# GpSimd gathers in bursts of four blocks in the message stage of a graph network

## The chip, the cores and the metric

The kernel runs on one core of a Trainium2 chip. The metric is the device time of one execution in microseconds (us). The kernel before took 2001.14 us (median of three runs, 1994.20 to 2003.65).

## The reference

Two graph layers with a mixture-of-experts layer behind each, on 3125 nodes of 256 numbers. The stage that is changed here is the message passing of the second graph layer. For each of 53,125 edges it takes the source node's row of `y`, multiplies it by weights of the edge, and adds the products up at the destination node:

```python
xg0 = y0[edge_src]
xg1 = y1[edge_src]
mid0 = w_a * xg0 * ea0
mid1 = w_b * jnp.einsum('euc,ec->eu', xg1, ea1) * INV_SQRT3
mid2 = (w_c * xg0)[:, :, None] * ea1[:, None, :]
mid3 = (w_d * ea0)[:, :, None] * xg1
mids = jnp.concatenate([mid0, mid1, mid2.reshape(-1, 3 * MUL), mid3.reshape(-1, 3 * MUL)], axis=1)
agg = jax.ops.segment_sum(mids, edge_dst, num_segments=n)
```

The edges are sorted by destination, so a run of neighbouring edges adds into a few neighbouring nodes.

## The kernel before

The program is a chain of stages that follow each other on all engines: a first summing stage (`sum`), the first node update, the first experts, a table stage that writes `y_dram`, the message stage (`msg`, the function `sum_messages`), the second update and routing, and the second experts.

**Tiles.** The nodes are cut into 25 tiles of 125. The sorted edges are cut into 208 blocks (`NB`) of 256. A block that lies across the border of two tiles belongs to both, so there are 208 + 25 - 1 = 232 pairs of a tile and a block (`NPAIR`). One step of the stage works on two pairs, so there are 116 steps (`NST`). Pair n belongs to block n - t when its tile is the t-th counted from 0. The first pair takes block 0, the last (n = 231, t = 24) block 207; a step uses 208/116 = 1.79 new blocks in the mean.

**A step on the engines.** SP loads the edge weights `w` of the two blocks (L1916), one load a pair. VectorE (DVE in the profile) makes a 0/1 mask of which edge goes to which node (L1993), then the products of gathered rows and weights (L2010, L2012: six instructions), then adds the sums of the step three earlier into `agg` (L2022, two instructions). ScalarE (ACT) scales the mask by the edge attributes, twelve instructions (L1961). TensorE (PE) multiplies masks and products into PSUM, which is the segment sum (L1978, L1982).

**Gathers.** GpSimd (POOL) fetches the rows of `y` that a block needs, with two indirect DMAs of 128 rows of 1 KB for each block (L1940), into a ring of 32 slots (`got`). The two DMAs of a block add 32 to that slot's semaphore `got_in` when they have landed. Behind each block POOL writes a small tile (`rest`, L1945).

**What sets the order.** The loop of each engine is written out by hand, and each engine runs its own list in order. These semaphores matter here:

- `blocks_in` is the number of blocks that have been counted as landed. POOL raises it in `arrived` (L1931 to L1934), after waiting for the blocks' `got_in`. DVE's products of a step wait until it reaches the number that the step needs (L2004).
- `made` is the number of steps whose products are done. POOL waits for it before it issues block b > 7 (L1938): steps 0 to (b - 6)//2 - 1 must be done. SP's loads of `w` wait for it too (L1909).
- `summed` is the number of steps that TensorE has finished. DVE's mask of step s waits for step s - 4 (L1992), its adds for theirs (L2018).

In the kernel before, POOL counts two blocks after it has issued two more: behind block b = 3, 5, 7, ... it waits for blocks b - 3 and b - 2, and it counts the last two at the end (L1946 to L1948).

Of the kernel before, what the change touches and what calls it, by code (L numbers as in the profile page):

```python
# [27 lines left out]
NB = -(-E // SB)  # L28
# [1836 lines left out]
def sum_messages(nc, k):  # L1865


    RING, LAG = 32, 3
    assert NB % 2 == 0
    AHEAD = RING - T  # L1870
    assert LAG + 2 < AHEAD
    RS, MB, ZB, XB = 4, 4, 6, 3
    LAST = NPAIR // 2 - 3
    assert LAST % RS == LAST % MB == 1 and LAST % XB == 2
# [3 lines left out]
    with Phase(nc, "msg") as ph:  # L1878
# [20 lines left out]
        w_in, got_in, blocks_in = ph.sems("w_in", RS), ph.sems("got_in", RING), ph.sem("blocks_in")  # L1899
# [5 lines left out]
        @block.sync  # L1905
        def _(sp):
            for s in range(NST):
                if s >= RS:
                    sp.wait_ge(made, s - RS + 1)  # L1909
                    sp.wait_ge(scaled_made, s - RS + 1)  # L1910
                if s == 1:
                    sp.wait_ge(k.x_put, 32 * (NG - 1))
                for h in range(2):
                    n = 2 * s + h
                    need = sp.value_load(k.pair_need[0:1, n:n + 1], min_val=1, max_val=NB)
                    sp.dma_start(w[s % RS][:, KC * h:KC * h + KC, :].rearrange("p u w -> p (u w)"),  # L1916
                                 k.edge_w[ds((need - 1) * SB, SB), :].rearrange("(p u) w -> p (u w)", u=KC)).then_inc(w_in[s % RS], 16)
            sp.wait_ge(raw_zero, 1)
            w00, w01, w10, w11 = k.L1_gnn_lin2_w00, k.L1_gnn_lin2_w01, k.L1_gnn_lin2_w10, k.L1_gnn_lin2_w11
            for q, (wa, wb) in enumerate([(w00, w11), (w11, w11), (w01, w10), (w10, w10)]):  # L1920
                sp.dma_start(raw[0:MUL, q, 0:MUL], wa).then_inc(raw_in, 16)
                sp.dma_start(raw[MUL:128, q, MUL:128], wb).then_inc(raw_in, 16)
            sp.wait_ge(summed, LAST + 1)
            for i in range(1, NG):
                for a, b in SPANS:
                    sp.dma_start(k.x_sb[a:b, i * G:i * G + G, :], k.x_dram[i * W:i * W + W, :].rearrange("(j p) d -> p j d", p=P)[a:b, :, :])\
                      .then_inc(k.x_back[i], 16)

        @block.gpsimd
        def _(pool):  # L1930
            def arrived(first, second):  # L1931
                for b in (first, second):
                    pool.wait_ge(got_in[b % RING], (b // RING + 1) * 16 * KC)
                pool.sem_inc(blocks_in, 2)  # L1934

            for b in range(NB):
                if b > AHEAD:
                    pool.wait_ge(made, (b - AHEAD + 1) // 2)  # L1938
                for u in range(KC):
                    pool.indirect_dma_start(  # L1940
                        got[:, (b + 1) % RING, u, :, :].rearrange("p k v -> p (k v)"), None, k.y_dram,
                        bass.IndirectOffsetOnAxis(ap=k.block_src[:, b, u:u + 1].bitcast(U32), axis=0)).then_inc(got_in[b % RING], 16)
                if b >= 1:
                    pool.wait_ge(rested, b)
                pool.memset(rest[:, :], 0.0).then_inc(rested, 1)  # L1945
                if b % 2 == 1 and b >= 3:  # L1946
                    arrived(b - 3, b - 2)
            arrived(NB - 2, NB - 1)  # L1948

        @block.scalar  # L1950
        def _(act):
# [517 lines left out]
def build(nc, inputs, out, stop=99):  # L2469
# [8 lines left out]
    with ExitStack() as ctx:  # L2478
# [58 lines left out]
        with ExitStack() as held:  # L2537
            k.agg = held.enter_context(nc.sbuf_tensor("agg1", [128, T, 2 * D], F32))
            k.up_w = held.enter_context(nc.sbuf_tensor("up_w", [128, 4, 128], F32))
            k.x_back = [nc.alloc_semaphore(f"x_back{i}") for i in range(NG)]  # L2540
            sum_messages(nc, k)
            m = Experts(nc, held, "ffn1", 8, 1, 1024, last=True)
            k.wd = held.enter_context(nc.sbuf_tensor("wd", [128, m.n, m.hid // 128, D], F32))
            k.wd_in = nc.alloc_semaphore("wd_in")
            k.row_stored = [nc.alloc_semaphore(f"row_stored{r}") for r in range(HR)]
            update_and_route(nc, k, m)
            m.hold_weights(nc, held)
            pick_slots(nc, k, m, k.L1_ffn_bd)
            run_second_experts(nc, k, m)
# [19 lines left out]
```

## Time and profile before

| what | value |
|---|---|
| runs, median (lowest to highest) | 2001.14 us (1994.20 to 2003.65) |
| profiled execution, span of its instructions | 2413.3 us |
| message stage in the profile, 1248 to 2057 us | 809 us |
| VectorE busy in it | 524.84 us |
| TensorE busy in it | 627.66 us, at 0.84 of the full clock |
| GpSimd busy in it | 441.23 us |

For the profiled execution the page gives the span from its first to its last instruction, and no other time of it; that span is 412.2 us longer than the median of the runs. How to read the views: "busy" is the time in which an engine executes; waits, branches and the issuing of hardware-queue DMAs are not counted. In a timeline each row is an instruction or a merged run of equal ones, with its start, its length, and in brackets the idle time of its engine just before it and what ended that. "issue" there means that the engine waited for nothing that the profile shows, "remote" that the semaphore was raised by an instruction whose record is missing. The clock column is the granted clock of TensorE, 1.00 for 2.4 GHz and 0.50 for 1.2 GHz.

### The profile page before, as it was taken

How to read it: one execution, taken by the hardware profiler on the slowest of the kernel's cores; microseconds unless marked ns; L12 is line 12 of the kernel's file. 1: busy time of each engine (PE TensorE's matmuls, PEld its weight loads, DVE VectorE, ACT ScalarE, POOL GpSimd, SP SyncE). 2: the span in 40 equal slices, each digit the busy share in tenths (PEclk: the TensorE clock that was granted, in tenths of full speed). 3: DMA queues.
4: the chain of work that ended last, by engine and by line, in shares of the span. 5: the costliest groups of instructions: out<-in, count | busy, mean ns of one | idle time of the engine just before them, and what ended most of it. 6: DMA issues, size and time to landing. Idle time of an engine off the chain costs nothing. (4 is left out here: it accounts for less than half of the span.)

```text
span 2413.3 us, 38460 instructions
## 1 busy us (share of the span) xinstructions
PE 1891.3 (78%) x9911; PEld 1517.9 (63%) x9911; DVE 1125.8 (47%) x2791; ACT 1021.4 (42%) x3052; POOL 1104.5 (46%) x1499
## 2 busy tenths in 40 slices
PE   1368787877799858999455877787778789899699
PEld 1245454554466657999335766676767679777588
DVE  3532222222242374544664666565656669431322
ACT  2513343343353532333264555454545557454222
POOL 5547667666700004555375665565655550000243
PEclk7679999889999858999777888887888889999799
DMA  5636556565734026666544554555554553255553
GB/s 150 202 90 198 190 187 198 185 193 187 210 140 138 11 64 201 212 212 215 135 149 147 150 159 140 151 155 145 147 153 144 150 148 107 69 164 177 155 180 129
DMA packets 229197, 376.43 MB, mean 156 GB/s; under 512 B 66081, under 2 KB 114308, under 8 KB 228998
## 3 DMA queue, kind: packets, MB, share of 16 engines
q1 hardware_dynamic: 174820, 222.13, 31.0%
q0 software_dynamic: 52224, 150.15, 20.2%
q8 instruction: 89, 1.46, 0.2%
q10 hardware_dynamic: 1954, 1.79, 0.2%
q14 instruction: 110, 0.90, 0.1%
HBM read 275.38 MB, written 99.57 MB: 155 GB/s over the span
## 5 line engine op out<-in xcount | busy, mean ns | idle before, releaser
L1940 POOL DMA_INDIRECT msg_got<-y_dram,block_src x416 | 412.4, 991 | 293.5 <-DVE msg_prod L2012 139.7
L439 POOL DMA_INDIRECT ffn_w<-xn_dram,block_src x384 | 364.6, 949 | 219.2 <-issue 81.7
L1961 ACT ACTIVATE msg_scaled<-msg_plain,msg_w 128x125 f32<-128x125 f32 x1044 | 314.0, 386 | 280.1 <-DVE msg_plain L1993 234.6
L554 PE MATMUL sum_ps_bank<-ffn_w,sum_onehot 128*125 x928 | 270.5, 419 | 115.6 <-DVE sum_onehot L893 84.3
L554 PEld LDWEIGHTS sum_ps_bank<-ffn_w,sum_onehot 128*125 128x125 f32 x928 | 184.0, 206 | 264.6 <-issue 246.6
L881 DVE TENSOR_TENSOR agg<-sum_ps_bank,agg 125x256 f32 x232 | 98.4, 424 | 432.4 <-PE sum_ps_bank L554 216.5
L541 PE MATMUL sum_ps_bank<-sum_fc,sum_space 128*128 128x512 f32 x416 | 231.9, 644 | 68.9 <-ACT sum_space L639 48.3
L650 ACT ACTIVATE sum_space<-sum_ps_bank,sum_rec 128x128 f32<-128x128 f32 x416 | 131.0, 369 | 330.4 <-PE sum_ps_bank L541 159.5
L1982 PE MATMUL msg_ps_z<-msg_prod,msg_scaled 128*125 128x128 f32 x1416 | 207.5, 293 | 53.7 <-issue 53.0
L1982 PEld LDWEIGHTS msg_ps_z<-msg_prod,msg_scaled 128*125 128x125 f32 x1416 | 198.6, 206 | 72.4 <-issue 64.1
L2022 DVE TENSOR_TENSOR agg<-msg_ps_z,agg 125x512 f32 x232 | 159.4, 687 | 23.9 <-issue 5.2
L1978 PE MATMUL msg_ps_z<-msg_prod,msg_plain 128*125 128x256 f32 x472 | 142.1, 420 | 31.9 <-issue 20.0
L2439 POOL DMA_INDIRECT last_rows<-ffn_rows,ffn_token x32 | 30.8, 963 | 289.2 <-SPq L78 279.7
L1533 ACT ACTIVATE ffn_run_hid<-ffn_run_ps_h,cols 128x128 f32<-128x128 f32 x256 | 73.2, 368 | 178.9 <-issue 134.6
L1993 DVE TENSOR_TENSOR msg_plain<-msg_ps_lanes,pair_dst 128x500 f32<-128x500 f32 x87 | 58.5, 672 | 190.6 <-remote 183.6
L1961 ACT ACTIVATE x_sb<-x_sb 128x125 f32<-128x125 f32 x348 | 104.0, 385 | 93.4 <-DVE x_sb L1993 77.2
L541 PEld LDWEIGHTS sum_ps_bank<-sum_fc,sum_space 128*128 128x128 f32 x416 | 76.0, 205 | 93.5 <-ACT sum_space L639 53.8
L1490 PEld LDWEIGHTS ffn_run_ps_h<-ffn_run_rows_t,ffn_run_w 128*128 128x128 f32 x1024 | 125.9, 194 | 5.0 <-DVE ffn_run_rows_t L1575 1.8
L1490 PE MATMUL ffn_run_ps_h<-ffn_run_rows_t,ffn_run_w 128*128 128x128 f32 x1024 | 126.6, 277 | 1.0 <-DVE ffn_run_rows_t L1575 1.0
L1982 PE MATMUL msg_ps_z<-x_sb,msg_scaled 128*125 128x128 f32 x672 | 100.1, 292 | 29.9 <-issue 29.7
L1504 PE MATMUL ffn_run_ps_r<-ffn_w,ffn_run_hid 128*128 x512 | 121.0, 379 | 0.0
L2012 DVE TENSOR_TENSOR msg_prod<-msg_w,msg_got 128x384 f32<-128x384 f32 x236 | 120.2, 550 | 0.0
(343 smaller groups left out, 3397.9 us busy)
## 6 DMA issues: line engine op xcount, KB each, us to landing
edge_w<-sum_space SPq DMA_DIRECT2D x52, 1040.0 KB
msg_w<-edge_w SPq DMA_DIRECT2D x174, 260.0 KB
ffn_run_w<-in_L_ffn_w SPq DMA_DIRECT2D x64, 512.0 KB
x_sb<-edge_w SPq DMA_DIRECT2D x58, 260.0 KB
ffn_rows<-agg SPq DMA_DIRECT2D x25, 448.0 KB
ffn_w<-in_L_ffn_w SPq DMA_DIRECT2D x16, 512.0 KB, 8.7
wd<-in_L_ffn_Wd SPq DMA_DIRECT2D x8, 1024.0 KB, 8.6
msg_got<-y_dram,block_src POOLq DMA_INDIRECT x416
```

The lines of the kernel that those rows point to most:

```text
L439: pool.indirect_dma_start(got[:, (b + 1) % RING, u, :], None, k.x if b < RAW else k.xn_dram, bass.IndirectOffsetOnAxis(ap=k.block_src[:, b ...
L541: pe.matmul(ps_w[q % WB][:, :, :].rearrange("p u d -> p (u d)"), hid[g % 2][:, b, :], fc2[:, :, :, :].rearrange("p u k v -> p (u k v)"), s ...
L554: last = pe.matmul(ps_sum[n % ZB][0:P, :], onehot[n % OB][:, u, :], got[:, ds(need % RING, 1), u, :].rearrange("p o d -> p (o d)"), start= ...
L650: act.activation(to[:, b, u, 0:128], ps_w[q % WB][:, u, 0:128], ACT.Copy, scale=r[:, b, u, 8:9])
L1490: last = pe.matmul(ps_h[b][c // 4][:, c % 4, :], w1[s][:, q, c * 128:(c + 1) * 128], rows_t[b][:, q, :], start=(q == 0), stop=(q == 1))
L1504: last = pe.matmul(ps_r[b][:, :], hid[b][:, c, :], m.w2[:, ds(e, 1), c, :].rearrange("p o d -> p (o d)"), start=(c == 0), stop=(c == HC - 1))
L1940: pool.indirect_dma_start(got[:, (b + 1) % RING, u, :, :].rearrange("p k v -> p (k v)"), None, k.y_dram, bass.IndirectOffsetOnAxis(ap=k.bl ...
L1961: last = act.activation(scaled[s % MB][:, x, c, :], plain[s % MB][:, c, :], ACT.Copy, scale=w[s % RS][:, c, D + x:D + x + 1])
L1978: pe.matmul(z[0:P, 0:4, :], mask[:, c, :], p[:, c, 0:4, :], start=(u == 0), stop=False, skip_group_check=True)
L1982: last = pe.matmul(z[0:P, 4:6 + x:1 + x, :], by[:, x, c, :], p[:, c, 4 + x:8:3 - x, :], start=False, stop=(x == 2 and u == KC - 1), skip_g ...
L2012: last = dve.tensor_tensor(p[:, at, 3 * q - 2:3 * q + 1, :], v[:, at, q:q + 1, :].to_broadcast([128, KC, 3, MUL]), y[:, :, 1:4, :], ALU.mult)
L2022: dve.tensor_tensor(row(k.agg, tile), ps_z[n % ZB][0:P, :, :].rearrange("p k v -> p (k v)"), row(k.agg, tile), ALU.add)\
```

## The change

POOL's loop now issues four blocks (eight gathers), waits until all four have landed, and counts the four together. The wait and the count behind every second block are gone, and so is the separate count at the end. The gather instructions, their number and their order stay; the semaphore `made` is waited for as before.

```diff
-    RING, LAG = 32, 3
-    assert NB % 2 == 0
+    RING, BURST = 32, 4
+    assert NB % BURST == 0
...
-            def arrived(first, second):
-                for b in (first, second):
+            def arrived(blocks):
+                for b in blocks:
                     pool.wait_ge(got_in[b % RING], (b // RING + 1) * 16 * KC)
-                pool.sem_inc(blocks_in, 2)
+                pool.sem_inc(blocks_in, len(blocks))
...
-                if b % 2 == 1 and b >= 3:
-                    arrived(b - 3, b - 2)
-            arrived(NB - 2, NB - 1)
+                if b % BURST == BURST - 1:
+                    arrived(range(b - BURST + 1, b + 1))
```

On POOL, blocks 6 and 7 and the start of block 8 read as follows in the kernel before. Semaphores are reused from stage to stage and stand here under names of an earlier stage: `sum_consts` and `sum_iota_made` are `got_in` of blocks 2 and 3, `sum_eps_made` and `sum_agg_zero` those of blocks 4 and 5, `sum_r_rstd_done` is `made`, `sum_r_stats_done` is `rested`.

```order
L1940 DMA msg_got<-y_dram,block_src 128x256 [waits sum_consts,sum_iota_made]
L1940 DMA msg_got<-y_dram,block_src 128x256
L1945 MEMSET msg_rest 128x32 [waits sum_r_stats_done]
L1940 DMA msg_got<-y_dram,block_src 128x256 x2
L1945 MEMSET msg_rest 128x32 [waits sum_r_stats_done]
L1940 DMA msg_got<-y_dram,block_src 128x256 [waits sum_eps_made,sum_agg_zero,sum_r_rstd_done]
```

So block 6 waits for blocks 2 and 3, and block 8 waits for blocks 4 and 5 while 6 and 7 are still under way. In the changed kernel the same place on POOL reads as follows; `sum_spare_zero` and `sum_tail_zero` are `got_in` of blocks 6 and 7.

```order
L1940 DMA msg_got<-y_dram,block_src 128x256 x2
L1945 MEMSET msg_rest 128x32 [waits sum_r_stats_done]
L1940 DMA msg_got<-y_dram,block_src 128x256 x2
L1945 MEMSET msg_rest 128x32 [waits sum_r_stats_done]
L1940 DMA msg_got<-y_dram,block_src 128x256 [waits sum_spare_zero,sum_tail_zero,sum_eps_made,sum_agg_zero,sum_r_rstd_done]
```

Block 6 waits for no landing any more, and block 8 waits for the landing of blocks 4 to 7, of which block 7 was issued just ahead of it. There are 52 such places, one behind each burst; in the last one it is the end of POOL's loop that waits.

## Rows read from the trace of the kernel before

**Rows 1.** Busy time by stretch: start:end, length, engines, clock, DMA share, GB/s

```profile
core 0: us, PE busy (x) PEld busy (x) DVE busy (x) ACT busy (x) POOL busy (x), PEclk, DMA share, GB/s
160.00:690.00 530.00, 424.65 (x1563) 271.31 (x1564) 154.25 (x366) 208.92 (x729) 344.37 (x507) 0.93 0.60 189
940.00:1100.00 160.00, 160.00 (x1116) 151.15 (x1116) 86.20 (x282) 49.18 (x172) 86.38 (x86) 1.00 0.66 212
1248.00:2057.00 809.00, 627.66 (x3714) 557.91 (x3714) 524.84 (x1047) 423.57 (x1393) 441.23 (x624) 0.84 0.51 149
1976.00:2045.00 69.00, 69.00 (x509) 65.40 (x509) 66.67 (x136) 53.99 (x182) 3.66 (x6) 1.00 0.40 111
```

**Rows 2.** Waits in the message stage: who, for whom, us in total, times, longest

```profile
DVE msg_plain L1993 <- remote: 183.6, 32, 18.9
POOL msg_got L1940 <- DVE msg_prod L2012: 139.7, 30, 7.6
POOL msg_got L1940 <- DVE x_sb L2012: 59.9, 13, 5.4
POOL msg_got L1940 <- DMA msg_got<-y_dram,block_src: 0.5, 3, 0.2
```

**Rows 3.** Timeline, 1274 to 1278 us: TensorE, ScalarE and GpSimd while gathers run

```profile
1274.03 0.40 ACT L1961 ACTIVATE msg_scaled<-msg_plain,msg_w 128x125 f32<-128x125 f32 x1 [0.99 <-issue]
1274.34 0.95 POOL L1940 DMA_INDIRECT msg_got<-y_dram,block_src  x1 [0.17 <-issue]
1274.74 0.37 PE L1982 MATMUL msg_ps_z<-msg_prod,x_sb 128*125 128x128 f32 x1 [2.52 <-issue]
1277.54 0.37 PE L1982 MATMUL msg_ps_z<-msg_prod,x_sb 128*125 128x128 f32 x1 [2.43 <-issue]
```

**Rows 4.** Mask instructions (L1993) from 1976 us on: ns, first and last start

```profile
L1993 DVE TENSOR_TENSOR msg_plain<-msg_ps_lanes,pair_dst x11: 668/668/679, 1981.4 to 2040.8; 128x500 f32<-128x500 f32 x11
L1993 DVE TENSOR_TENSOR x_sb<-msg_ps_lanes,pair_dst x4: 668/668/679, 1976.7 to 2031.7; 128x500 f32<-128x500 f32 x4
```

**Rows 5.** Waits of GpSimd's gathers in the first stage, 150 to 700 us

```profile
POOL ffn_w L439 <- remote: 56.7, 32, 2.0
POOL ffn_w L439 <- PE sum_ps_bank L554: 33.1, 19, 7.2
```

**Rows 6.** Timeline: first gather, first products, last products, last adds

```profile
1248.67 1.04 POOL L1940 DMA_INDIRECT msg_got<-y_dram,block_src  x1 [3.06 <-POOLq L82]
...
1257.32 0.42 DVE L2010 TENSOR_TENSOR msg_prod<-msg_w,msg_got 128x256 f32<-128x256 f32 x1 [0.89 <-issue]
...
2045.37 0.41 DVE L2010 TENSOR_TENSOR msg_prod<-msg_w,msg_got 128x256 f32<-128x256 f32 x1
...
2055.43 1.53 DVE L2022 TENSOR_TENSOR agg<-msg_ps_z,agg 125x512 f32 x2 [1.37 <-PE msg_ps_z L1982]
```

**Rows 7.** Timeline: GpSimd over four blocks, DVE's release, a later gather

```profile
1604.04 0.95 POOL L1940 DMA_INDIRECT msg_got<-y_dram,block_src  x1 [5.33 <-DVE x_sb L2012]
...
1613.23 0.95 POOL L1940 DMA_INDIRECT msg_got<-y_dram,block_src  x1 [0.30 <-issue]
...
1617.75 1.02 DVE L2012 TENSOR_TENSOR msg_prod<-x_sb,msg_got 128x384 f32<-128x384 f32 x2
...
1619.04 0.95 POOL L1940 DMA_INDIRECT msg_got<-y_dram,block_src  x1 [4.73 <-DVE msg_prod L2012]
...
1842.20 0.95 POOL L1940 DMA_INDIRECT msg_got<-y_dram,block_src  x1 [0.30 <-issue]
```

**Rows 8.** DMA view, 1614.2 to 1617.2 us: GB/s in 40 equal slices

```profile
GB/s 219 218 273 273 55 0 0 0 0 273 0 164 382 273 109 219 164 164 0 0 0 0 0 0 0 0 0 0 0 0 0 0 0 0 0 0 0 218 0 0
```

**Rows 9.** DMA view, 1843.2 to 1846.2 us, behind the gather of 1842.20 us

```profile
GB/s 222 194 250 166 277 387 332 360 333 221 166 221 275 275 166 111 192 301 164 164 164 109 55 0 0 55 0 0 55 0 0 0 0 0 0 0 0 0 218 0
q1 hardware_dynamic: 133, 0.24, 22.9%
```

More of the change, by code:

```diff
@@ L1865, in sum_messages @@
 def sum_messages(nc, k):
-    RING, LAG = 32, 3
-    assert NB % 2 == 0
+    RING, BURST = 32, 4
+    assert NB % BURST == 0
     AHEAD = RING - T
-    assert LAG + 2 < AHEAD
+    assert BURST + 2 < AHEAD
     RS, MB, ZB, XB = 4, 4, 6, 3
```

## The prediction

> **What bounds the kernel now.** I read the busy times by stretch first, to see what the message stage costs and which engine is full there: 809 us, in which no engine is [rows 1]. Then the waits, for the gathers of GpSimd and the masks of VectorE; the reader is to see that waiting for a landing costs GpSimd 0.5 us in the whole stage, while it waits 139.7 + 59.9 = 199.6 us in 43 places for VectorE's products, and that VectorE's longest wait is at the mask, whose only semaphore is `summed` [rows 2]. So in the profile GpSimd is early, and TensorE late. Then the timeline, to see what keeps TensorE: nothing that it waits for. While gathers run, it starts one matmul in 2.80 us (1274.74 to 1277.54) with "issue" ahead of it, and ScalarE sits idle 0.99 us before an instruction in the same way, in the middle of twelve equal ones; GpSimd beside them keeps its even pace [rows 3]. Last the end of the stage, where the gathers are over but all else goes on: TensorE is busy 69 of 69 us at the full clock, and VectorE 66.67 [rows 1]. Its 15 masks from 1976.7 to 2040.8 stand 64.1/14 = 4.58 us apart [rows 4]. A step therefore costs 4.58 us once TensorE is not held; in the stage as profiled it costs 809/116 = 7.0.
>
> That makes one question decide the forecast: is TensorE held in this way in the timed runs too? The profiled span is 2413.3 us and the median 2001.1, so 412 us of the span are not in a timed run. They cannot come from stretches that are full: from 940 to 1100 us TensorE is busy without a gap [rows 1]. The two places with long gather traffic can give them. In the first stage GpSimd waits 56.7 + 33.1 = 89.8 us beyond its own pace [rows 5]. In the message stage, at 4.58 us a step, the stretch from the first gather (1248.67) would take: 8.65 us to the first products (1257.32), 115 steps of 4.58 (526.7), and 11.59 from the last step's products (2045.37) to the end of the last adds (2056.96), so 547 us instead of 808.3 [rows 4, 6]. That is 261 less; with the 89.8 it is 351 of the 412. Were the stage held in the timed runs as in the profile, 322 us would have to be found elsewhere, which no row offers. I infer, and cannot show, that the holding belongs to the profiled execution, and take the stage at 547 us in a timed run. GpSimd is then nearly even with VectorE: four blocks take it 10.14 us (1604.04 to 1614.18), 10.44 with the gap of 0.30 that follows [rows 7], and VectorE needs four blocks in 4/1.79 = 2.23 steps, or 10.2 us. Where GpSimd sets the pace that is up to 0.24 us x 52 = 12 us more; I take 550 us, with 547 and 559 as ends.
>
> **The change part by part.** Removed: the wait and count behind each second block. They cost nothing now (0.5 us, [rows 2]), since a block counted there was issued two blocks earlier, 5 us or more before. Nothing is gained by their going; waits and counts are the same in number or fewer, and lie in gaps of 0.17 us between gathers.
>
> Added: 52 waits for the block issued just ahead. Queued behind each on GpSimd are the gathers of the next burst, and behind those VectorE's products, which wait for the count. SP's loads of `w` hang on `made`, so they are late by as much as VectorE, but not ahead of it. The trace of before never shows this wait. From both sides: the gather that starts at 1613.23 ends at 1614.18, and the gather traffic behind it stops with slice 18 of 40 of a 3 us view (0.075 us each), 1.4 us on [rows 7, 8]; behind the gather that ends at 1843.15 traffic stops with slice 29, apart from a lone packet in slice 38, 2.2 us on, with 133 packets of a hardware queue beside it [rows 7, 9]. I take 1.9 us: the middle of the two, because loads of `w` run beside some bursts and not beside others, and 0.1 that I guess for the semaphore, which comes after the last packet. Then GpSimd has to start again: after VectorE's release (1617.75 + 1.02 = 1618.77) its gather began at 1619.04, 0.27 us on [rows 7].
>
> A burst thus takes 10.14 + 1.9 + 0.27 = 12.31 us for four blocks, against the 10.2 us in which VectorE uses them. So GpSimd becomes what the stage waits for, and VectorE stands still some 2.1 us a burst. The semaphore `made` does not bind on top: block 4k + 2 wants 2k - 2 steps done, which were released a burst earlier and take VectorE 9.2 of 12.31 us.
>
> The sum: 51 full bursts are 627.8 us, the last one to its landing 12.04, so the last blocks are counted 639.8 us after the first gather. They are wanted by the last two steps: 4.58 us for step 114, and 11.59 from the products of step 115 to the end. That is 656 us, against 550 now: 106 us more, or 2001.1 + 106 = 2107 us. With the landing at 1.4 us it is 630 (+80), at 2.3 it is 677 (+127); with the stage before at 547 or 559, 3 more or 9 less.
>
> TensorE's clock: in the first stage, where TensorE also pauses between groups, the granted clock is 0.93 [rows 1]. At the full clock TensorE needs at most 4.58 us a step, 10.2 us a burst; at 0.93 it needs 11.0, still under 12.31. So I add nothing for it.
>
> The Trainium skill (DMA: Bandwidth & Descriptors, Rules for kernel authors) says to issue a DMA early and wait for it late, so that its fixed cost is hidden; the change does the reverse for the fourth block of each burst. Its section on the anatomy of a GpSimd DMA gives about 2.0 us plus bytes over 436 GB/s, an estimate of 2.3 us for the 128 KB of one gather from its issue; that is 1.35 us behind the 0.95 of the instruction, and the sum by it would be 28 us less, 2079. The trace shows 1.4 to 2.2 us to the last packet alone, so the trace is used.
>
> **Rivals.**
> No change: the holding of TensorE is in the timed runs as well. Then GpSimd's 199.6 us of waiting for products cover 52 x (1.9 + 0.27) = 113 us of landings, and VectorE goes on waiting for `summed`. Time 2001, say 1991 to 2011. For it: it is what the trace literally shows. Against it: the missing 412 us. The change would then do what it says, and be hidden.
>
> Partly covered: a timed stage between the two, at 600 us before (5.2 us a step). GpSimd's own 656 stays, so +56 and 2057. For it: the 61 us of the 412 that I could not place show that my account is not closed; they speak for other stages as much as for this one.
>
> Faster: the count comes sooner. Now a landed pair is counted only once two more blocks are issued, and where GpSimd is stopped by `made` ahead of these (43 times, 4.6 us each [rows 2]), landed blocks stay uncounted; after the change they are counted when they land. If VectorE's waits hang on the count, each of those places gives up to 4.6 - 1.9 - 0.27 = 2.5 us, 43 x 2.5 = 107 us at most, 1894, and half of it 1948. It decides from the point where VectorE waits for `blocks_in` and GpSimd for `made` in turn. Against it: the waits of VectorE stand before the mask, which does not wait for the count.
>
> **How the numbers follow.** Forecast 0.72, its own range 2070 to 2135 (landing 1.4 to 2.3 us, stage before 547 to 559, and some 10 us for what the semaphore adds behind the last packet). Partly covered 0.11, no change 0.12, faster 0.05. About 0.5% (10 us) is what a measurement of this kernel can tell from no change. Slower by more than that: the forecast, the partly covered case, and a little of the no-change case: 0.84; within it 0.11; faster 0.05. The range of 8 in 10 takes the forecast and the partly covered case whole, 2020 to 2140. Predicted 2107.
>
> **What would show it.** Right: in the new profile the gathers come in groups of eight with a gap of 1.5 to 2.5 us behind each, ended by the landing of `msg_got`, 52 times, and GpSimd's wait for the products is all but gone. The timed runs are slower by far more than the profile is, since the profiled stage before had 199.6 us of cover. Each gap's length is the landing, and each 0.1 us in it is 5 us of time. Wrong: if GpSimd still waits for `made` in the timed regime, the cover was there, and the time stays; if the gaps are near 1 us, a burst takes 11.1 us and the stage some 596; if TensorE's clock stands at 0.50 through much of the bursts, TensorE needs up to 20 us a burst and the time passes 2140.

## The result, and the profile after

The changed kernel takes 2182.72 us (median of four runs, 2175.62 to 2183.90), against 1997.67 for the kernel before in the same comparison: ratio 1.092 (95% interval 1.089 to 1.095), 185 us more. 2107 us was forecast, with 2140 as the upper end. The direction and the mechanism were right; the price of one wait was put at 2.17 us, and the trace has 3.69.

The profiled execution that the rows of before come from was itself slower than the timed runs (2413.3 us against some 2000), so I compare with a second profile of the same kernel, e1 below, whose span is 1995.1 us. The profile of the changed kernel has a span of 2173.9 us and belongs to a run of 2175.6.

Busy time of the message stage, from the first gather to the last add, in the second profile of the kernel before and then in the changed kernel (the columns are those of [rows 1]):

```profile
1078.80:1639.00 560.20, 531.53 (x3713) 487.86 (x3712) 523.47 (x1046) 420.80 (x1393) 446.90 (x624) 0.99 0.73 214
```

```profile
1074.00:1814.00 740.00, 580.69 (x3714) 536.30 (x3713) 525.49 (x1047) 421.15 (x1393) 449.49 (x624) 0.89 0.56 163
```

The stage grew by 180 of the 185 us. VectorE, ScalarE and GpSimd have nearly the same busy time in both; TensorE's is longer at a lower clock (0.89 in place of 0.99). What was added is idle time. The stretches ahead of the stage and behind it are alike: 1078.8 and 356 us in the one, 1074 and 359 in the other.

Waits of GpSimd's gathers and of VectorE's first product instruction (L2009, formerly L2010) in the changed kernel; who, for whom, us in total, times, longest:

```profile
POOL msg_got L1940 <- DMA msg_got<-y_dram,block_src: 177.1, 50, 4.7
DVE msg_prod L2009 <- issue: 120.6, 27, 5.4
DVE x_sb L2009 <- issue: 56.5, 14, 5.6
POOL msg_got L1940 <- DVE msg_prod L2011: 0.5, 3, 0.2
```

GpSimd waits 177.1 us for landings; in the second profile of the kernel before it is 3.1 us (its row stands under e1). The 199.6 us of waiting for products and VectorE's 183.6 us ahead of the mask [rows 2] are all but absent from both profiles (0.5 us are left), so the change did not remove them. VectorE now stands still ahead of the products, where it waits for the count. One burst's end on GpSimd, in the timeline of the changed kernel:

```profile
1414.33 0.95 POOL L1940 DMA_INDIRECT msg_got<-y_dram,block_src  x1 [0.17 <-issue]
1415.59 0.95 POOL L1940 DMA_INDIRECT msg_got<-y_dram,block_src  x1 [0.30 <-issue]
1416.54 0.14 POOL L1945 MEMSET msg_rest<- 128x32 f32 x1
1420.53 1.25 POOL L1940 DMA_INDIRECT msg_got<-y_dram,block_src  x1 [3.86 <-DMA msg_got<-y_dram,block_src]
```

From the end of the last gather (1416.54) to the next one (1420.53) it is 3.99 us. Over 51 such gaps the mean is 3.69 us, and a burst itself takes 10.23 us in the mean; both are worked out from all the gather rows. On GpSimd's queue the second of two waiting instructions, with the count, stands 0.78 us ahead of that next gather, from start to start (view of line 1934: 43 ns long, started at 1419.8, which is 1419.76 before rounding):

```profile
L1934 POOLq EVENT_SEMAPHORE  x1: 43/43/43, 1419.8 to 1419.8; - x1
```

VectorE's products follow the count at 1420.06, ahead of the gather:

```profile
1420.06 0.43 DVE L2009 TENSOR_TENSOR x_sb<-x_sb,msg_got 128x256 f32<-128x256 f32 x1 [4.83 <-issue]
```

How long a gather is under way, from the start of its instruction to its landing, in the second profile of before and in the changed kernel (minimum, median, maximum). The profiles have the landing of only 50 and 114 of the 416 gathers, so the small difference between the two medians is not shown to be one; with the same order of gathers, e8 below has a median of 3.7:

```profile
DMA to landing us min/median/max: 2.7/3.4/4.6
```

```profile
DMA to landing us min/median/max: 2.8/3.8/5.1
```

The gap itself splits more surely, because each of the 51 gaps of the changed kernel has the last packet of the gathers and the last step of their semaphores in its trace. In the mean the last packet ends 2.39 us behind the last gather's end, and the last semaphore step comes 0.40 us later: 2.79 us to the landing, where 1.9 was forecast. From there to the start of the next gather, with the waits and the count in it, it is 0.90 us, where 0.27 was forecast.

### The profile page after: what moved, and what is told of

Read it like the earlier page. It is cut to its first block and busy times, and to the rows that moved or that the text cites. A ratio compares the mean times of both kernels' runs of the same rounds, so it can differ in the third digit from the quotient of the medians.

```text
span 2173.9 us, 38460 instructions
## 1 busy us (share of the span) xinstructions
PE 1807.3 (83%) x9911; PEld 1480.0 (68%) x9911; DVE 1127.4 (52%) x2791; ACT 1021.5 (47%) x3052; POOL 1111.9 (51%) x1499
## 5 line engine op out<-in xcount | busy, mean ns | idle before, releaser
L1940 POOL DMA_INDIRECT msg_got<-y_dram,block_src x416 | 420.6, 1011 | 274.0 <-DMA msg_got<-y_dram,block_src 177.1
L554 PEld LDWEIGHTS sum_ps_bank<-ffn_w,sum_onehot 128*125 128x125 f32 x928 | 173.1, 194 | 190.5 <-issue 174.3
L554 PE MATMUL sum_ps_bank<-ffn_w,sum_onehot 128*125 x928 | 255.3, 401 | 49.9 <-DVE sum_onehot L893 27.9
L541 PE MATMUL sum_ps_bank<-sum_fc,sum_space 128*128 128x512 f32 x416 | 211.5, 593 | 1.3 <-ACT sum_space L639 1.3
L1981 PEld LDWEIGHTS msg_ps_z<-msg_prod,msg_scaled 128*125 128x125 f32 x1416 | 191.0, 204 | 8.7
L1981 PE MATMUL msg_ps_z<-msg_prod,msg_scaled 128*125 128x128 f32 x1416 | 190.3, 288 | 0.0
L1977 PEld LDWEIGHTS msg_ps_z<-msg_prod,msg_plain 128*125 128x125 f32 x472 | 88.0, 208 | 99.6 <-issue 89.6
L1595 POOL DMA_INDIRECT ffn_results<-ffn_run_res,ffn_place x64 | 66.4, 1038 | 101.8 <-DVE ffn_run_res L1554 101.8
L2399 PE MATMUL last_ps_r<-wd,last_hid_t 128*128 x512 | 117.2, 383 | 0.0
```

What stands on the lines that cost most here:

```text
L541: pe.matmul(ps_w[q % WB][:, :, :].rearrange("p u d -> p (u d)"), hid[g % 2][:, b, :], fc2[:, :, :, :].rearrange("p u k v -> p (u k v)"), s ...
L554: last = pe.matmul(ps_sum[n % ZB][0:P, :], onehot[n % OB][:, u, :], got[:, ds(need % RING, 1), u, :].rearrange("p o d -> p (o d)"), start= ...
L1940: pool.indirect_dma_start(got[:, (b + 1) % RING, u, :, :].rearrange("p k v -> p (k v)"), None, k.y_dram, bass.IndirectOffsetOnAxis(ap=k.bl ...
L1977: pe.matmul(z[0:P, 0:4, :], mask[:, c, :], p[:, c, 0:4, :], start=(u == 0), stop=False, skip_group_check=True)
L1981: last = pe.matmul(z[0:P, 4:6 + x:1 + x, :], by[:, x, c, :], p[:, c, 4 + x:8:3 - x, :], start=False, stop=(x == 2 and u == KC - 1), skip_g ...
L2399: last = pe.matmul(ps_r[n % 2][:, 0:D], hid_t[n % 2][:, c, :], k.wd[:, ds(e, 1), c, :].rearrange("p o d -> p (o d)"), start=(c == 0), stop ...
```

## The experiments

All times are medians beside runs of the kernel before on the same chip (1995.4 us in the first group, e1 to e4; 1995.1 in the second, e5 to e9). There was no e7.

### e1: the kernel before, profiled again

No edit.

> The kernel before, unchanged, for a second profile of it. In the first one the span was 2413 us against 1998 us in the runs, and TensorE started single matmuls with nothing to wait for; in the profile of the changed kernel the span (2173.9) and the run (2175.6) agree. Theory: that holding belonged to one profiled execution; a second profile has a span near 1996 us, the message stage takes some 563 us (1998 less the 1074 ahead of the stage and the 359 behind it in the changed kernel's profile), VectorE's step is 4.6 us, and GpSimd waits for no landing. Rival: the old order of gathers itself holds TensorE, and the span is near 2400 us again.

Measured: 1996.66 us, ratio 1.000 (0.999 to 1.002); the span is 1995.1. TensorE is busy 531.5 of 560.2 us in the stage, at 0.99 of the full clock. The 107 masks from 1099.6 to 1599.5 us are 4.72 us apart; I had 4.58. The first theory holds: the holding of TensorE in [rows 3] belonged to one profiled execution. What caused it there was not found. Waits of the gathers and of the first product instruction in this profile:

```profile
POOL msg_got L1940 <- issue: 94.5, 396, 0.3
POOL msg_got L1940 <- DMA msg_got<-y_dram,block_src: 3.1, 19, 0.2
DVE msg_prod L2010 <- issue: 5.6, 11, 1.5
DVE x_sb L2010 <- issue: 2.8, 6, 0.5
```

GpSimd waits for next to nothing but its own pace here, so there is no cover for a landing.

### e2: bursts of two

```diff
-    RING, BURST = 32, 4
+    RING, BURST = 32, 2
```

> The changed kernel with bursts of two blocks in place of four. Theory A, the landing: every burst costs the time from its last gather's end to the next gather, 3.7 us in the changed kernel's profile, 104 times in place of 52: 52 x 3.7 = 192 us more than the changed kernel, near 2370 us. Theory B, the coarse count: VectorE loses because it gets its blocks four at a time; two at a time is what the kernel before does, so the time goes back to 1998 to 2050 us.

Measured: 2351.88 us, ratio 1.179 (1.177 to 1.181). Twice as many landings are waited for, and the loss is 357 us in place of 185. The count by twos, as in the kernel before, does not bring the time back, so the coarse count is not the cause.

### e3 and e4: four counted together, one or two blocks later

```diff
-                if b % BURST == BURST - 1:
-                    arrived(range(b - BURST + 1, b + 1))
+                if b % BURST == 0 and b >= BURST:
+                    arrived(range(b - BURST + 1 - 1, b + 1 - 1))
+            arrived(range(NB - BURST, NB))
```

This is e3; in e4 the condition is `b % BURST == 1 and b >= BURST` and the range `(b - BURST + 1 - 2, b + 1 - 2)`.

> Four blocks are still counted together, but the wait for them stands behind one further block, so that one block (2.5 us of issuing) is under way in the wait. Theory A: 3.7 - 2.5 = 1.2 us of each wait is left, a burst takes 10.1 + 1.2 = 11.3 us, 52 of them 588 us and the stage some 605: 45 us over the kernel before, near 2043 us. Theory B: the count is as coarse as in the changed kernel, and the time stays near 2180 us.

> Four blocks are counted together, and the wait for them stands behind two further blocks (5 us of issuing). Theory A: the wait is over before it begins, GpSimd runs at its own 2.5 us a block, and the time is that of the kernel before, 1995 to 2015 us. Theory B: near 2180 us.

Measured: e3 2026.09 us, ratio 1.017 (1.014 to 1.019); e4 2000.46 us, ratio 1.003 (1.001 to 1.005). With two blocks issued over the wait, the count by fours costs some 5 us; with one, 31; with none, 185. So it is not that four are counted together, but that the youngest is waited for. In e3 I had expected 1.2 us to be left at each wait, and 45 us in all. Three waits in its timeline:

```profile
1299.73 1.25 POOL L1940 DMA_INDIRECT msg_got<-y_dram,block_src  x1 [1.14 <-DMA msg_got<-y_dram,block_src]
...
1310.56 1.25 POOL L1940 DMA_INDIRECT msg_got<-y_dram,block_src  x1 [0.60 <-issue]
...
1321.44 1.27 POOL L1940 DMA_INDIRECT msg_got<-y_dram,block_src  x1 [0.34 <-issue]
```

Where there is nothing to wait for, 0.17 us stand there. Some waits are left with 1.1 us, some with next to nothing; over all 51 of them the mean is 0.52 us above that, or 26 us.

### e5: one semaphore for a burst

```diff
-                for b in blocks:
-                    pool.wait_ge(got_in[b % RING], (b // RING + 1) * 16 * KC)
+                k4 = blocks[0] // BURST
+                pool.wait_ge(got_in[k4 % (RING // BURST)], (k4 // (RING // BURST) + 1) * 16 * KC * BURST)
...
-                        ...).then_inc(got_in[b % RING], 16)
+                        ...).then_inc(got_in[b // BURST % (RING // BURST)], 16)
```

> The changed kernel, but the eight gathers of a burst raise one semaphore, and GpSimd waits once for 128 in place of four times for 32. In the changed kernel's trace 0.9 us pass between the last landing and the next gather. Theory: it is the four waits and the count, each some 0.09 us by the distance of two such rows: three waits fewer give 52 x 0.27 = 14 us, near 2168 us. Rival: the first three waits are over while the fourth block is still landing, and the 0.9 us lie in the start of GpSimd itself: no change, 2178 to 2188 us.

Measured: 2171.34 us, ratio 1.089 (1.086 to 1.091), 11 us below the changed kernel, which ran in another comparison (1.092, 1.089 to 1.095); the intervals overlap. The mean gap fell from 3.69 to 3.58 us, or 6 us over 52. In the build the four waits were two waiting instructions, so there was one to save, not three. Of the 0.90 us from the landing to the next gather, 0.78 stay without it, and 0.76 of these lie between the start of the instruction with the count and the next gather. So the second theory is nearer: it is the start of GpSimd itself. In e1 the same instruction has nothing to wait for, and the gather starts 0.12 us behind it in all 103 places; in all 51 places of the changed kernel, where GpSimd has stood still, it is 0.78 to 1.08.

### e6: little weight traffic

```diff
-                    sp.dma_start(w[s % RS][:, KC * h:KC * h + KC, :].rearrange("p u w -> p (u w)"),
-                                 k.edge_w[...].rearrange("(p u) w -> p (u w)", u=KC)).then_inc(w_in[s % RS], 16)
+                    rows = 128 if s < RS else 16
+                    sp.dma_start(w[s % RS][0:rows, KC * h:KC * h + KC, :].rearrange("p u w -> p (u w)"),
+                                 k.edge_w[...].rearrange("(p u) w -> p (u w)", u=KC)[0:rows, :]).then_inc(w_in[s % RS], 16)
```

> The changed kernel, with the loads of the edge weights cut to 16 of 128 partitions from step 4 on (old weights stay in the rest), so that the weight traffic beside the gathers falls to an eighth. In the changed kernel the last packet of a burst lands 2.4 us behind the last gather's end. Theory: the weight loads hold it up, and without them it comes after 1.4 us as in the quietest view of the kernel before: 52 x 1.0 = 52 us less, near 2131 us. Rival: the landing takes this long by itself, 2183 us.

From step 4 on this kernel leaves out seven eighths of each weight load, and so does not compute the same sums.

Measured: 2136.51 us, ratio 1.071 (1.068 to 1.073), 46 us below the changed kernel. Its gathers, and their waits:

```profile
DMA to landing us min/median/max: 2.7/2.9/4.1
```

```profile
POOL msg_got L1941 <- DMA msg_got<-y_dram,block_src: 136.8, 50, 3.9
```

The median of the known landings falls from 3.8 to 2.9 us. Over all 51 gaps the mean falls from 3.69 to 2.88 us, the last packet from 2.39 to 1.61 us behind the last gather's end. So about 0.8 us of a gap is the weight loads beside it: 52 x 0.81 = 42 of the 46 us. The remaining 1.98 us to the landing, and the 0.90 behind it, are there without them.

### e8 and e9: without the small write behind each block

```diff
-                if b >= 1:
-                    pool.wait_ge(rested, b)
-                pool.memset(rest[:, :], 0.0).then_inc(rested, 1)
```

e8 is the kernel before with this edit, e9 the changed kernel.

> The kernel before without the small write (L1945) and its wait behind each block on GpSimd, 0.31 us of 2.62 us a block. GpSimd then needs 208 x 2.3 = 480 us for the stage in place of 544, and VectorE with 116 x 4.58 = 531 us sets the pace alone. Theory: both set the pace in turn in the kernel before, so up to 9 us go (560 to 551), 1987 to 1994 us. Rival: gathers that follow each other more closely get into the way of the weight loads, no gain or some loss.

> The changed kernel without that small write and its wait. If GpSimd's chain of issuing, landing and starting again sets the stage's pace, 0.31 us go from each of 208 blocks: 64 us less, near 2118 us. If VectorE's handling of four blocks at a time sets it, the time stays near 2183 us. If the landing only begins when the transfers of all eight gathers are through, the wait grows by what the issuing lost, and the gain is less than half, over 2150 us.

Measured: e8 1995.19 us, ratio 1.000 (0.998 to 1.001); e9 2177.80 us, ratio 1.091 (1.088 to 1.094). Neither tells the theories apart, because the edit took no time away. Gathers of e9:

```profile
1399.99 0.97 POOL L1940 DMA_INDIRECT msg_got<-y_dram,block_src  x1 [0.30 <-issue]
1401.27 0.95 POOL L1940 DMA_INDIRECT msg_got<-y_dram,block_src  x1 [0.30 <-issue]
1402.52 0.95 POOL L1940 DMA_INDIRECT msg_got<-y_dram,block_src  x1 [0.30 <-issue]
```

They still start 1.25 to 1.28 us apart. The write had been lying in a gap of 0.30 us that stands between any two gathers: with it 0.14 + 0.17, without it 0.30. That e9 stays near the 2183 of its second theory, and over the 2150 of its third, says nothing for either.

### All in one view

The profile's line of the gathers in e1, the changed kernel, e2, e3, e4, e5 and e6, in this order: count, busy us, mean ns, then GpSimd's idle time just before them in us, and what ended most of it.

```profile
L1940 POOL DMA_INDIRECT msg_got<-y_dram,block_src x416 | 418.1, 1005 | 100.7 <-issue 94.5
```

```profile
L1940 POOL DMA_INDIRECT msg_got<-y_dram,block_src x416 | 420.6, 1011 | 274.0 <-DMA msg_got<-y_dram,block_src 177.1
```

```profile
L1940 POOL DMA_INDIRECT msg_got<-y_dram,block_src x416 | 427.1, 1027 | 443.8 <-issue 430.5
```

```profile
L1940 POOL DMA_INDIRECT msg_got<-y_dram,block_src x416 | 419.4, 1008 | 127.1 <-issue 102.0
```

```profile
L1940 POOL DMA_INDIRECT msg_got<-y_dram,block_src x416 | 419.4, 1008 | 100.7 <-issue 96.3
```

```profile
L1940 POOL DMA_INDIRECT msg_got<-y_dram,block_src x416 | 419.3, 1008 | 270.5 <-DMA msg_got<-y_dram,block_src 172.1
```

```profile
L1941 POOL DMA_INDIRECT msg_got<-y_dram,block_src x416 | 420.1, 1010 | 232.8 <-DMA msg_got<-y_dram,block_src 136.8
```

Idle time over e1's 100.7, from one profiled execution each, and median run time over the kernel before of the same comparison:

| kernel | idle added, us | time added, us |
|---|---|---|
| e4, two later | 0 | 5 |
| e3, one later | 26 | 31 |
| e6, little weight traffic | 132 | 141 |
| e5, one semaphore | 170 | 176 |
| changed kernel | 173 | 185 |
| e2, bursts of two | 343 | 357 |

The time follows GpSimd's idle time nearly one to one, in six kernels. (For e2 this view puts the waits under "issue", where it knew no landing that ended them.) GpSimd's chain sets the pace of the stage, and the landing, with the start behind it, is what was added to it.

## Why the prediction was wrong, and where it was right

Right, by its own steps:

- *The cover.* I inferred from the missing 412 us that TensorE is not held in the timed runs, and put the stage at 550 us. It is 560 (e1). The rivals "no change" and "partly covered" rested on a cover that was not there.
- *The place.* GpSimd waits 50 times for the landing, and VectorE for the count. `made` does not bind: 0.5 us in three places.
- *The rival "faster".* VectorE hardly waits for the count in the kernel before: 5.6 + 2.8 us of "issue" ahead of its products in e1 against 120.6 + 56.5 in the changed kernel. (In that rival 4.6 - 1.9 - 0.27 is 2.43, not 2.5, and 43 of them are 104 us, not 107; nothing else hangs on it.)
- *TensorE's clock.* I added nothing for it. It fell from 0.99 to 0.89 in the stage, and the one-to-one relation above leaves some 12 us for it and all else.

Wrong: the term of the added wait, "I take 1.9 us" for the landing and 0.27 for the start. Together 2.17 us a burst; the trace of the changed kernel has 3.69, and gaps from 2.81 to 4.83 where I had named 1.5 to 2.5 as the sign of being right. The working with the measured sizes closes: 656 us, plus 52 x (2.79 - 1.9) = 46 for the landing, 52 x (0.90 - 0.27) = 33 for the start, 52 x (10.23 - 10.14) = 5 for the burst, is 740 us, and the stage measures 740. Less 560 that is 180, not 106.

Why each was too small:

- *The last packet.* I took 1.8 us, the middle of 1.4 and 2.2, because loads of `w` run beside some bursts and not beside others. In the profile that I read this is so: they moved over 150 KB beside the last gather's packets in 20 of the 41 gaps of over 2.3 us, and the last packet ended 1.87 us behind the gather in these and 1.53 in the 20 with under 50 KB. In the changed kernel they did so in 48 of 51 gaps, and the mean over all is 2.39. So the middle was the wrong choice, and even the loaded gaps of the slowed execution were too short. e6 shows what the weight loads are worth: 1.61 us with an eighth of them.
- *The semaphore.* I guessed 0.1 us for what follows the last packet; over the 51 gaps of the changed kernel the last recorded step of the semaphores comes 0.40 us behind it.
- *The start.* The 0.27 us in [rows 7] were between VectorE's release and a gather that stood next on the queue and itself waited for `made`. In the changed kernel the gather stands behind separate waiting instructions and the count, and begins 0.78 us behind the last of them, 0.90 behind the landing. e5 shows that their number hardly matters, and e1 that the instruction itself need not cost it (0.12 us). Why the start takes so long after a standstill there was not tried further.

The Trainium skill (DMA: Bandwidth & Descriptors, Rules for kernel authors) has the advice to issue a DMA early and wait for it late, and the series agrees with it: waiting two blocks late costs 5 us, one block late 31, not late 185. The estimate of 2.3 us for a gather of 128 KB, worked out from the Trainium skill's fit (DMA: Bandwidth & Descriptors, Anatomy of one DMA — SWDGE (gpsimd) path), is short of the traces: medians of 2.9 us with little traffic beside it (e6), 3.4 to 3.8 with the kernel's own (e1, changed kernel).

The range also failed by its upper end: both readings of the landing, 1.4 and 2.2 us, came from the slowed execution that I had already declared untypical, and the start had no range at all.

## What to carry to other kernels

In this kernel, GpSimd issues transfers in order, and where it waits for its youngest one it pays the whole time to landing and the start of the next transfer, and starts no other transfer meanwhile. Let such an engine wait for transfers that lie as many issues back as a landing takes. Here two blocks of 2.5 us cover 3.7 us, one does not. And when a profile's span is far from the run time, the durations in it that depend on load (a landing, a queue) belong to that slower execution as much as its waits do: use it for lengths of instructions (the gather's 0.95 us held), and take the durations that depend on load at the upper end, or from a second profile.

## What was not expected of the hardware

- Indirect gathers of 128 rows started a median of 1.26 us apart on GpSimd with a 0.14 us write between every second pair (changed kernel, gaps at the waits left out) and 1.27 without it (e9): mostly 0.95 us and a gap of 0.30.
- The next gather began 0.78 us behind the instruction with the count where GpSimd had stood still for it (changed kernel), and 0.12 us where it had not (e1).
- The first gather after a wait was often longer, 1.25 us in place of 0.95; the mean over the bursts' first gathers of the changed kernel is 1.23 us. The busy time of all 416 grew from 418.1 to 420.6 us only.
- In one profiled execution TensorE and ScalarE started one instruction in 1.4 to 2.8 us while gathers ran [rows 3], and in the next profile of the same kernel they did not. The runs did not show the cause.
